# Constant products in the waits of a tail, an earlier table load, and two scores in the drain of a Fourier tower

## The reference

```
h = concat(grid, x) @ P_w + P_b                          # 32 channels
for i in range(4):
    out_modes = einsum(rfft2(h)[:16, :16], spec[i])      # 16 x 16 modes
    h = leaky(irfft2(out_modes) + conv3x3(h, conv_w[i]) + conv_b[i])
h = leaky(h @ Q1_w + Q1_b) @ Q2_w + Q2_b                 # one value a pixel: (32, 64, 64)
h = h + attention(layernorm(h), W)                       # 64 tokens of 64 values an image
h = h + ffn(layernorm(h))
```

## Time and profile before

| | |
|---|---|
| three runs | 1138.23, 1141.36, 1144.83 us |
| the profiled execution | 1145.78 us, its span 1144.0 us |
| busy shares of the span | PE 92%, PEld 49%, DVE 53%, ACT 40%, POOL 13% |
| mean granted clock of TensorE | 0.974 (1.00 is 2.4 GHz, 0.50 is 1.2 GHz) |
| chain that ended last | PE 84%, DVE 7%, issue 5%, ACT 3% |

### The profile page before, as it was taken

One profiled execution on the slowest core, in us unless ns is written; L12 is line 12 of the kernel. 1 busy time (PEld: TensorE's weight loads), 2 busy tenths in 40 slices (PEclk: granted clock), 3 DMA queues, 4 the chain that ended last, 5 costly groups with the idle time before them and its releaser, 6 DMA issues.

```text
span 1144.0 us, 48520 instructions
## 1 busy us (share of the span) xinstructions
PE 1056.8 (92%) x22416; PEld 557.0 (49%) x22416; DVE 611.4 (53%) x564; ACT 460.1 (40%) x889; POOL 152.4 (13%) x298
## 2 busy tenths in 40 slices
PE   4899998899999999899999998999999999799965
PEld 2555544555555554655555555434443434366712
DVE  4777787655555656555556665111223313387743
ACT  1255555323333333133333332334344443566523
POOL 2022111011111111011111111112111121300000
PEclk8999999999999999999999999999999999799986
DMA  9377668379889888589889886768774642000001
GB/s 317 109 204 185 176 167 228 109 209 260 248 244 268 247 214 245 149 237 261 254 263 260 242 228 164 180 145 187 166 173 111 148 97 68 8 1 1 2 0 19
DMA packets 64987, 194.34 MB, mean 170 GB/s; under 512 B 22064, under 2 KB 22832, under 8 KB 57392
## 3 DMA queue, kind: packets, MB, share of 16 engines
q1 hardware_dynamic: 52496, 138.25, 45.2%
q0 software_dynamic: 12288, 52.97, 16.2%
HBM read 138.19 MB, written 52.95 MB: 167 GB/s over the span
## 4 chain that ended last, share of the span: by engine, by line
PE 84%; DVE 7%; issue 5%; ACT 3%; DMA 0%; DVEq 0%; ACTq 0%
PE psum L633 16%; PE psum L619 14%; PE psum L665 11%; PE psum L647 7%; PE psum L591 6%; PE psum L604 5%; PE psum L539 4%; PE psum L526 4%; PE psum L683 3%; PE psum L576 2%; PE psum L879 2%; PE psum L691 1%; DVE xt L1237 1%; DVE ft L1244 1%; PE psum L890 1%
## 5 line engine op out<-in xcount | busy, mean ns | idle before, releaser
L1058 ACT ACTIVATE x_now<-psum,conv_bias 128x512 f32<-128x512 f32 x256 | 155.3, 692 | 327.2 <-PE psum L647 248.4
L1269 DVE STREAM_TRANSPOSE vt<-psum 128x1024 f32<-128x1024 f32 x64 | 126.6, 1978 | 205.1 <-PE psum L591 205.1
L1237 DVE STREAM_TRANSPOSE xt<-x_now 128x1024 f32<-128x1024 f32 x100 | 202.8, 2067 | 15.4 <-ACT x_now L1058 8.9
L1244 DVE STREAM_TRANSPOSE ft<-psum 128x1024 f32<-128x1024 f32 x50 | 100.5, 2010 | 189.8 <-PE psum L526 189.8
L633 PE MATMUL psum<-halo,conv 64*32 64x512 f32 x3072 | 189.5, 593 | 4.9 <-issue 4.8
L336 ACT ACTIVATE spec<-psum 32x128 f32<-32x128 f32 x372 | 143.8, 386 | 94.6 <-PE psum L539 90.8
L619 PE MATMUL psum<-halo,conv 128*128 128x512 f32 x384 | 178.0, 605 | 0.7 <-ACT x_now L1058 0.7
L470 POOL DMA_DIRECT2D activations<-x_now x192 | 94.3, 492 | 616.0 <-PE psum L633 410.4
L665 PEld LDWEIGHTS psum<-dft,vt 64*64 64x64 f32 x8192 | 126.5, 135 | 50.8 <-issue 50.7
L665 PE MATMUL psum<-dft,vt 64*64 64x64 f32 x8192 | 136.3, 220 | 2.6 <-issue 2.5
L619 PEld LDWEIGHTS psum<-halo,conv 128*128 128x128 f32 x384 | 68.6, 189 | 83.3 <-issue 73.8
(11 more groups left out here) (150 smaller groups left out, 787.4 us busy)
## 6 DMA issues: line engine op xcount, KB each, us to landing
halo<-activations SPq DMA_DIRECT2D x768, 132.0 KB, 3.5
activations<-x_now POOLq DMA_DIRECT2D x192, 264.0 KB, 4.2
wspec<-in_spec SPq DMA_DIRECT2D x64, 256.0 KB, 5.8
xcol<-in_xcol SPq DMA_DIRECT2D x16, 384.0 KB, 5.8
x_now<-in_ser SPq DMA_DIRECT2D x2, 1056.0 KB, 6.9
spec<-in_onehot SPq DMA_DIRECT2D x8, 256.0 KB, 6.0
wspec<-in_causal SPq DMA_DIRECT2D x8, 256.0 KB, 6.5
consts<-in_tail SPq DMA_DIRECT2D x1, 1481.0 KB, 13.8
```

The costliest lines, as they stand in the source:

```text
L1058: copy(x_now[:, k, 16 * u:16 * u + 16, 0:G], acc[u].rearrange("p (i j) -> p i j", j=G), ACT.Prelu, bias=conv_bias[:, l:l + 1], alpha=SLOPE ...
L1237: vec.transpose(xt[:, 32 * m:32 * m + 32, :], x_now[:, n % 2, :, 0:G].rearrange("p (i m) j -> p m j i", m=2)[:, m]).then_inc(s_xt, 1)
L1244: vec.transpose(ft[:].rearrange("p k c -> p c k"), rowed.rearrange("p a b -> p (a b)").rearrange("p (i c) -> p c i", c=C)).then_inc(s_ft, 1)
L1269: vec.transpose(vt[:, k].rearrange("p h r o -> p (h r) o").rearrange("p y o -> p o y"), backed.rearrange("p a b -> p (a b)").rearrange("p ...
```

## The change

- `stay_busy` now takes a bank and multiplies the constant `fc1` by itself (128 x 128); it is called in three places of the tail: 24 products into bank 2 behind `fold_resid(0)`, 12 into bank 0 behind `variance(1)`, and 12 into bank 0 behind `variance(3)`. Nobody reads the results.
- A logarithm of one column (`eps`) stands on ScalarE between squares 0 and 1, and between squares 2 and 3.
- `head_activate(LAST, 0)` and `(LAST, 1)` come ahead of the last pair's third slot, and so ahead of the root of M1.
- The scores of images 0 and 1 stand between `head_hidden(LAST, 0)` and `head_hidden(LAST, 2)` on TensorE; the loop makes scores from i = 2 on. VectorE's first subtraction waits for `head_out(LAST)` (`s_y`).
- The host sets `p["eps"]` a few lines earlier.

```diff
-            def stay_busy(n):
+            def stay_busy(to, n):
                 for _ in range(n):
-                    mm(spare[:, 0:128], fold_w[:, 0, :], fold_w[:, 0, :], start=True, stop=True)
+                    mm(bank(to)[:, 0:128], cst["fc1"], cst["fc1"], start=True, stop=True)
...
             fronts_read(LAST, 0, 1, 2)
             head_hidden(LAST, 0)
+            scores(0)
+            scores(1)
             head_hidden(LAST, 2)
             head_out(LAST)
...
             for i in range(B + 3):
-                if i < B:
+                if 2 <= i < B:
                     scores(i)
...
             fold_resid(0)
+            stay_busy(2, 24)
             pe.wait_ge(s_gs, 1)
...
             variance(1)
+            stay_busy(0, 12)
...
                 variance(2 + k)
+            stay_busy(0, 12)
...
                 if last and p > 0:
                     head_read(p - 1)
+                if T == NL * PAIRS - 1:
+                    head_activate(p, 0)
+                    head_activate(p, 1)
                 if last:
                     fronts(p, 2)
...
-            for u in range(4):
+            for u in range(2, 4):
                 head_activate(LAST, u)
...
             square(0)
+            copy(little[:, 5, 0:1], cst["eps"], ACT.Ln)
             square(1)
...
             square(2)
+            copy(little[:, 5, 1:2], cst["eps"], ACT.Ln)
             square(3)
...
                 link(vec.tensor_reduce(small[:, i % 2, 0:8], s4, AX.X, ALU.max))
+                if i == 0:
+                    dve.wait_ge(s_y, PAIRS)
```

More of the change, by code:

```diff
@@ L863, in _ @@
                         pair(l, p)
[L864 to L867, removed]
             def scores(i):
@@ L882, in scores @@
                 t.then_inc(s_sc, 1)
+            fronts_read(LAST, 0, 1, 2)
+            head_hidden(LAST, 0)
+            scores(0)
+            scores(1)
+            head_hidden(LAST, 2)
+            head_out(LAST)
             def turn_prob(j):
@@ L1580, in tail_inputs @@
     p["fc2"] = diag(t["L0_ffn_fc2_w"].T, 8)
+    p["eps"] = np.full((128, 1), 1e-8, np.float32)
     p["last"] = np.tile(np.concatenate([np.eye(64, dtype=np.float32), t["L0_ffn_fgate_w"].T], axis=1), (2, 1))
@@ L1583, in tail_inputs @@
         p[a] = col(t["L0_ffn_" + a])
-    p["eps"] = np.full((128, 1), 1e-8, np.float32)
     onehot = np.tile(np.eye(64, dtype=np.float32)[:, None, :], (1, B, NE)).reshape(64, B, NE * H)
```

## The result

The changed kernel takes 1133.88 us (median of six runs, 1127.53 to 1136.32), the kernel before 1141.85 (six runs, three of them those of the table ahead of the change). That is 8.0 us by the medians. The ratio of the runs is 0.9917, 95% interval [0.9889, 0.9946]: 9.5 us, between 6 and 13. The forecast of 1130 lies 4 us lower, its range of 1123 to 1137 holds the time. The profiled execution has a span of 1132.9 us against 1144.0.

What follows compares the result with a forecast made beforehand. TensorE, 92% busy, and in the drain and tail the serial handing round of work at a falling clock were taken as the bound; 6.9 + 1.5 + 0.7 + 2.2 + 0.4 + 1.75 = 13.5 us off gave 1130, range 1123 to 1137.

Steps and rivals of the forecast that it cites:

- Scores and activations in the drain: Last image pair's drain: scores fill TensorE's wait, activations start ahead of the root; gain 6.9 us, upper end 7.1.
- rival (a): Drain: the clock falls all the same, as three idle stretches follow one another; 2.4 to 4 us less, 1133; chance 0.25.
- 24 products: Tail, before the gates are repeated: they overrun by 1.8 us, but what follows runs at 2.4 GHz; gain 1.5 us.
- Logarithm's table: Tail, ScalarE: the table load moves between the squares; gain 0.7 us in the first place, 0.4 us in the second.
- rival (c): Tail squares: square isn't in the logarithm's table, each small logarithm costs three loads; 3.5 us less, 1133.5; chance 0.03.
- 12 products ahead of fc1: Tail, behind variance 1: if the clock holds, fc1 and half of fc2 run faster; gain 2.2 us, otherwise nothing.
- 12 products ahead of the last stage: Tail's end: weight loads follow the clock, so 32 records take 1.9 us instead of 3.68; gain 1.75 us.
- rival (b): Tail: the clock falls in one or both stretches before fc1 and the last stage; 2 to 4 us less, 1133; chance 0.17.
- Base: Whole kernel's starting time: profiled 1145.8 us gives 1132.3, median 1141.4 gives 1127.9; the middle, 1130, was taken.
- The rival on the other side: Constant products start at the low clock: 24 take 11.1 us and hold the repeats up; 1147; chance 0.03.

Runs made afterwards that it cites:

- the drain part alone: Only the two scores between the head halves, the two earlier activations and VectorE's new wait, put into the kernel before: 1139.56 us against 1145.82, ratio 0.995.

## Why the prediction was right, and where its sizes were off

- **Scores and activations in the drain.** The mechanism is right: with the clock up, the drain takes 100.62 us in two profiles of it unfilled, 6.7 us under the 107.34 that I started from, and 6.9 was the forecast. The likeliest case was not: the clock fell in four of the six profiles with this drain (102.89, 102.99, 103.37, 103.42), which is rival (a). It was priced at 2.4 us for a fall where it came, and cost 2.3 to 2.8. The sentence that fails is the one that compared each new idle stretch with one of 1.33 us that had left the clock up: here three follow one another with only 1.07 and 0.63 us of products between. That their sequence is the reason is argued, not shown. That baseline of 107.34 was itself a slow one; two other profiles of the same drain have 105.8 and 105.9, so against these the gain is 5.3 at best and 2.4 to 3.0 where the clock fell.
- **24 products.** Length (5.6 forecast, 5.62), overrun (1.8, 1.6), start of VectorE's products (7.7 us behind the residual, 7.72) and their end came out. The gain was 0.8 and not 1.5: the term mis-sized is TensorE's chain of experts, residual, repeat and variance behind it. I had 0.86 a step; at each change of what is read and written the step takes 1.05 to 1.12.
- **Logarithm's table.** 0.7 and 0.4 us forecast; 0.67 and 0.34 to 0.39 measured, alone and in the whole. Ten loads in the last 170 us before, ten after: no load stands between the small logarithm and the square behind it, so squares run with the logarithm's table, and rival (c) is out. The Trainium skill (ScalarE: Activation LUTs, What ACT_TABLE_LOAD costs) has 2.66 us a switch with its drain; here a load takes 1.28, and the activation starts 0.02 behind it.
- **12 products ahead of fc1.** The clock held in every profile that had them. 1.7 us up to the end of the centring, where 2.2 were forecast: the first ReLU starts 1.16 us behind fc1 and fc2 2.70, which I had at 1.0 and 2.4.
- **12 products ahead of the last stage.** 0.6 us of 1.75, since the clock fell within the stage (3.07 us; 2.97, 2.81, 2.46, 2.30 and once 2.01 in the others with 12 products; 2.01, 2.00 and 2.00 with 18). This is rival (b), in one of its two places. With 12 products the clock held through this stage in one profile of six, with 18 in three of three, which speaks for the idle stretch as the cause and isn't proof. With the clock up the 32 records take the 1.9 to 2.0 us that were forecast, and the loads 188 ns instead of 330. The Trainium skill's rule (TensorE: Matmul & The Clock Gate, LDWEIGHTS), columns / 1.2 ns for a load with no word on the clock, would have left 3.4 us for 32 loads one behind the other; the trace disagrees.
- **Base.** I took the middle between 1132.3 and 1127.9, by the profiled time and by the median. The tower's scatter of ten microseconds makes that choice worth nothing. The sum of 13.5 was 5.4 too large: the two clock falls (2.8 and 1.1 us), the two chains (0.7 and 0.5), and 0.2 in the rest of the drain. The base, 1143.5 with that sum, lay 1.7 above the measured median of 1141.85, and this hid a part of it: from 1141.85 the sum would have given 1128.4. That the forecast missed by 3.9 us and not 5.5 is luck.
- The rival on the other side, products at the low clock, didn't come: the 24 ran at 1.00 in every profile.

What stays open: what exactly brings the clock down in the changed drain where its waits are left empty. With the same work it held twice and fell four times, 7 to 10 us behind the first head product. In two of the four it fell at the idle stretch ahead of T2 (at 981.5 in the drain part alone, at 986.1 without the 24), in the other two within unbroken work, and each time it was low for 6.8 us. With products in the waits it held in all three profiles, which beside two of six without them isn't proof. No experiment moved the drain in time against the clock, so a rival is left: that the moment of the fall is chance, and the three were lucky.

## What to carry to other kernels

A constant product in a wait is worth the clock it keeps (2.4 us in the wait for the gates), and costs its overrun one for one where the wait ends on the path: size it from the wait's length and the measured 0.234 us a product, and let it end ahead of what it waits for. Moving a table load off the path gives only the distance to the next late input, so look for that input first, and put the load where the engine is idle already. Judge such edits by stages within a profile: each of these is worth 0.3 to 4 us, where runs of one kernel lie up to 14 apart.

## What the runs showed that I had not expected

- A drain with the same instructions takes 105.8 to 107.3 us in three profiles without its change and 100.6 to 103.4 in six with it, by how long the clock is low: 10.2 to 13.7 us in the three, 6.8 or not at all in the six.
- In the changed kernel's first profile the clock falls when TensorE has been busy for 1.5 us again, not while it is idle, and stays low for 6.8 us of unbroken work (985.5 to 992.3).
- Weight loads overlap: 32 loads of 188 ns for alternating row halves and their products of 68 columns take 2.01 us together, 63 ns each, and 48 full-height loads of 192 ns with products of 128 columns 5.62 us, 117 ns each. Whether the halves or the fewer columns make the difference no run shows.
